# Converting the expert weights piece by piece inside the tile loops, in a transformer layer with 32 routed experts

## The reference

```python
logits = x @ wg.T
scores = softmax(logits)                      # 4096 x 32
weights, idx = top_k(scores, 8)
weights = weights / sum(weights)
# rows sorted by expert, then for each expert e and its rows xs:
g = xs @ w1[e]            # 512 x 192
u = xs @ v1[e]            # 512 x 192
h = silu(g) * u
ys = h @ w2[e]            # 192 x 512
out = zeros().at[token].add(ys * weight)
x = x + layernorm(out)
```

## Time and profile before

| | us |
|---|---|
| median of 3 runs | 2524.11 |
| lowest and highest | 2519.49, 2526.7 |
| the profiled execution, its own time | 2532.36 |
| its span in the trace | 2530.7 |

### The profile page before, as it was taken

The page is one execution under the profiler, slowest core; times in us unless marked ns, Lnnn a source line. Parts: engine busy times, 40 slices in busy tenths (PEclk is TensorE's granted clock), DMA queues, the critical chain, the costliest instruction groups (busy, mean ns, idle before and its releaser), DMA issues.

```text
span 2530.7 us, 62483 instructions
## 1 busy us (share of the span) xinstructions
PE 2255.0 (89%) x11804; PEld 1911.8 (76%) x11805; DVE 1491.3 (59%) x4814; ACT 1228.2 (49%) x2635; POOL 947.9 (37%) x1126
## 2 busy tenths in 40 slices
PE   7999899999989999991798999988999898988990
PEld 5887588888868888880687878867889787977880
DVE  4455567777767777773545555555554555455546
ACT  3343456666556666651334444444444444444443
POOL 1112025555535555556133333323333232323342
PEclk9999999999999999995899999999999999999995
DMA  3234113333333323326798777777787777776778
GB/s 117 91 112 121 59 34 119 105 122 118 122 137 114 127 103 118 116 106 218 209 239 186 149 157 148 158 182 153 150 150 137 166 149 165 138 167 134 137 129 290
DMA packets 164700, 357.53 MB, mean 141 GB/s; under 512 B 21152, under 2 KB 21152, under 8 KB 164512
## 3 DMA queue, kind: packets, MB, share of 16 engines
q0 software_dynamic: 60224, 144.21, 28.9%
q1 hardware_dynamic: 90976, 173.32, 23.1%
q10 hardware_dynamic: 13440, 39.33, 4.8%
HBM read 177.65 MB, written 179.14 MB: 141 GB/s over the span
## 4 chain that ended last, share of the span: by engine, by line
PE 29%; DMA 8%; issue 7%; ACTq 4%; ACT 2%; DVE 2%; DVEq 2%; POOL 1%; SPq 1%; POOLq 0%
DMA moe_sum<-X,aidx 6%; PE bank L443 5%; PE bank L444 5%; PE bank L445 5%; PE bank L434 4%; PE bank L460 2%; PE bank L453 2%; PE bank L464 2%; PE bank L461 2%; PE bank L462 2%; PE bank L463 2%; ACTq L322 1%; ACT WB L500 1%; DMA LATE<-w_in 1%; ACTq L297 1%
## 5 line engine op out<-in xcount | busy, mean ns | idle before, releaser
L1442 POOL DMA_INDIRECT moe_sum<-X,aidx x274 | 425.0, 1551 | 855.9 <-issue 522.5
L922 PE MATMUL bank<-WB,XH 128*128 128x512 f32 x1536 | 478.0, 392 | 0.0
L443 PE MATMUL bank<-WB,XL 128*128 x1096 | 397.7, 363 | 5.0 <-DVE XL L695 4.9
L444 PE MATMUL bank<-WB,XH 128*128 x1096 | 371.6, 339 | 0.0
L445 PE MATMUL bank<-WB,XH 128*128 x1096 | 370.7, 338 | 0.0
L922 PEld LDWEIGHTS bank<-WB,XH 128*128 128x128 f32 x1536 | 290.5, 189 | 60.3 <-issue 0.5
L922 PE MATMUL bank<-WB,XL 128*128 128x512 f32 x768 | 316.5, 412 | 10.4 <-DVE XL L1229 10.4
L922 PE MATMUL bank<-WB,SH 128*128 128x512 f32 x1024 | 318.9, 393 | 0.0
L703 DVE SCALAR_TENSOR_TENSOR BIG<-BIG,bank x274 | 95.2, 347 | 353.8 <-issue 206.5
L1508 POOL DMA_INDIRECT sorted_rows<-srow,pos x256 | 265.4, 1037 | 95.4 <-issue 95.4
L521 ACT ACTIVATE X<-bank (+1 forms) x276 | 165.1, 598 | 224.7 <-PE bank L464 110.4
(11 more groups left out here) (205 smaller groups left out, 4259.4 us busy)
## 6 DMA issues: line engine op xcount, KB each, us to landing
BIG<-sorted_rows SPq DMA_DIRECT2D x276, 274.0 KB
X<-x_in SPq DMA_DIRECT2D x64, 256.0 KB, 2.8
RAW<-w_in ACTq DMA_DIRECT2D x15, 768.0 KB
LATE<-w_in ACTq DMA_DIRECT2D x15, 768.0 KB
sorted_rows<-BIG SPq DMA_DIRECT2D x33, 274.0 KB, 12.7
moe_sum<-LATE SPq DMA_DIRECT2D x34, 256.0 KB, 3.0
LATE<-x_in SPq DMA_DIRECT2D x32, 256.0 KB
RAW<-wo_in SPq DMA_DIRECT2D x16, 512.0 KB, 3.5
```

What stands on the lines that cost most here:

```text
L443: nc.tensor.matmul(eu[s][:, 0:UP], XL[:, s, k, :], wh, start=k == 0, stop=False)
L444: nc.tensor.matmul(eu[s][:, 0:UP], XH[:, s, k, :], wh, start=False, stop=False)
L922: last = nc.tensor.matmul(ps, w, m, start=start and i == 0, stop=stop and i == len(terms) - 1)
L1442: nc.gpsimd.indirect_dma_start(acc_dram[:, :], bass.IndirectOffsetOnAxis(aidx[:, s:s + 1], 0), rows, None, compute_op=ALU.add).then_inc(s_ ...
```

## The change

Each tile of expert e now also converts one piece of 512 columns of expert e+2's weights. The high parts become five pieces of 512 columns (w13 is 1536 columns wide and w2 gives two more pieces), and the layout of a set is such that the low part stands at a fixed distance from the high part. In ACT's tile loop, tile number k within the expert converts piece k & 3, every tile, also when all four have been converted. Behind the loop, ACT runs a second loop over the pieces from m to 4, where m is the smaller of the expert's tile number and 4, then a one-column activation that carries the semaphore `s_ehx`. DVE's tile loop subtracts one piece per tile, and behind its loop it waits for `s_ehx` and for its own pieces (`s_el`), runs a loop over the pieces from m to 3, with m at most 3, and the half piece that carries `s_elo`. Ahead of the tiles stands now `ready`: ACT waits for `s_elo`, issues the load of expert e+3 (three DMAs, since the half piece is loaded once), and waits until the weights of expert e+2 have landed.

The three table entries per expert become one packed word, from which first tile, number and m are taken by shifts. PE reads one word per tile in place of two, and waits before `up` until the low parts of its expert are done.

```diff
@@ each_expert @@
-                n = eng.value_load(table[0:1, 0, bass.ds(e, 1)], min_val=1, max_val=TOKENS // P + 1)
-                first = eng.value_load(table[0:1, 1, bass.ds(e, 1)], min_val=0, max_val=MAX_TILES)
-                convert(e, q)
-                body(e, q, first, n)
+                word = eng.value_load(table[0:1, row, bass.ds(e, 1)], min_val=512 + 32768, max_val=8 * 32768 - 1)
+                first, n, m = word & 511, (word >> 9) & 63, word >> 15
+                ready(e, q)
+                body(e, q, first, n, m)
@@ moe_pe @@
-            def up(g, s, off):
+            def up(g, s, e, off):
+                pe.wait_ge(s_elo, e + 1)
+                stand(pe)
                 pe.wait_ge(s_exl, g + 2)
                 pe.wait_ge(s_h, g + 1)
...
-                    before, now = slot_at(g), slot_at(g + 2)
+                    e, now, before = experts_at(g)
@@ moe_act @@
-            def convert(e, q):
-                if isinstance(e, int) and e + 2 >= EXPERTS:
-                    return
-                load = not (isinstance(e, int) and e + 3 >= EXPERTS)
-                before = act.value_load(table[0:1, 3, bass.ds(e, 1)], min_val=1, max_val=MAX_TILES + 3)
-                act.wait_ge(s_D, before)
-                stand(act)
-                if load:
+            def ready(e, q):
+                if not isinstance(e, int) or e + 3 < EXPERTS:
                     act.wait_ge(s_elo, e + 2)
                     stand(act)
-                for piece in range(len(PIECES)):
-                    weights_high(e + 2, (q + 2) % WSETS, q % 2, piece)
-                    if load and piece < 4:
-                        load_weights(act, e + 3, (q + 1) % 2, piece)
+                    load_weights(act, e + 3, (q + 1) % 2)
+                if converts(e):
+                    act.wait_ge(s_ewr[q % 2], (e - q % 2) * 24 + 96)
+                    stand(act)
...
                     rows_high(g + 2, same)
+                    if converts(e):
+                        weights_high(to, i, (k & (LOW_PIECES - 1)) * PIECE).then_inc(s_eh, 1)
+                with act.Fori(0, n) as k:
+                    tile(first + k, k)
+                if converts(e):
+                    with act.Fori(m, HIGH_PIECES) as k:
+                        weights_high(to, i, k * PIECE)
+                    all_high(e + 2)
@@ moe_dve @@
+                    if converts(e):
+                        dve.wait_ge(s_eh, g + (2 * HIGH_PIECES + 1))
+                        weights_low(to, i, (k & (LOW_PIECES - 1)) * PIECE).then_inc(s_el, 1)
...
+                if converts(e):
+                    dve.wait_ge(s_ehx, e + 3)
+                    stand(dve)
+                    dve.wait_ge(s_el, first + n)
+                    stand(dve)
+                    with dve.Fori(m, LOW_PIECES) as k:
+                        weights_low(to, i, k * PIECE)
+                    last_low(to, i)
@@ tables (DVE) @@
-            nc.vector.tensor_copy(table[:, 0:2, :], tn[0:1, 2:4, :])
-            nc.vector.memset(table[:, 3, 0:1], 1)
-            nc.vector.tensor_scalar(table[:, 3, 1:EXPERTS], tn[0:1, 3, 0:EXPERTS - 1], 3.0, None, ALU.add)
+            done(nc.vector.scalar_tensor_tensor(tn[0:1, 0, :], tn[0:1, 2, :], 512.0, tn[0:1, 3, :], ALU.mult, ALU.add))
+            for i in range(2):
+                done(nc.vector.tensor_scalar(words[:, i, :], tn[0:1, 2, :], float(HIGH_PIECES - 1 - i), 32768.0, ALU.min, ALU.mult))
+            settled()
+            for i in range(2):
+                nc.vector.tensor_tensor(table[:, i, :], words[:, i, :], tn[0:1, 0, :], ALU.add)
...
+            done(nc.vector.tensor_copy(iota_g[0:1, :], bank[6][0:1, 0:MAX_TILES]))
+            settled()
+            nc.vector.scalar_tensor_tensor(at_tile[:, 0, 2:MAX_TILES], iota_g[0:1, 0:MAX_TILES - 2], 64.0, iota_g[0:1, 2:MAX_TILES], ALU.mult, ALU.add)
```

More of the change, by code:

```diff
@@ L487, in moe_pe, with weights_high, all_high @@
             act_t(total - 1, 1)
-            down(total - 2, 0, slot_at(total))
-            down(total - 1, 1, slot_at(total + 1))
+            down(total - 2, 0, experts_at(total)[2])
+            down(total - 1, 1, experts_at(total + 1)[2])
         def moe_act(act):
             act.sem_inc(s_y, 2)
[L495 to L500, removed]
+            def weights_high(q, i, at_piece):
+                return nc.scalar.activation(WB[:, bass.ds(at_piece + q * WSET, PIECE)], raws[i][:, bass.ds(at_piece, PIECE)], ACT.Copy)
+            def all_high(e):
+                nc.scalar.activation(marks[:, bass.ds(e, 1)], mhalf[:, :], ACT.Copy).then_inc(s_ehx, 1)
             def rows_high(g, parity):
@@ L526, in moe_act @@
             act.wait_ge(s_q, 4 * TILES)
-            for piece in range(len(PIECES)):
[L528 to L532, removed]
+            for e in range(2):
+                act.wait_ge(s_ewr[e], 48)
+                for piece in range(HIGH_PIECES):
+                    weights_high(e, e, piece * PIECE).then_inc(s_eh, 1)
+                all_high(e)
+                if e == 0:
+                    act.wait_ge(s_elo, 1)
+                    load_weights(act, 2, 0)
             act.wait_ge(s_T, 3)
@@ L560, in tile @@
                     rows_high(g + 2, same)
-                with act.Fori(0, n) as i:
-                    tile(first + i)
-            total = each_expert(act, convert, body)
+                    if converts(e):
[6 more added lines that the diff above has]
+                    all_high(e + 2)
+            total = each_expert(act, 0, ready, body)
             act_high(total - 1, 1)
@@ L718, in add_index @@
                 nc.vector.tensor_copy(aidx[:, at(0, parity, 1, 1)], BIG[:, bass.ds(tail_at(g) + (WR + ID_COL - W_COL), 1)]).then_inc(s_aid, 1)
-            for piece in range(len(PIECES)):
-                weights_low(1, 1, 1, piece)
+            first_low(1)
             for i in range(2):
@@ L728, in moe_dve, with ready, body, tile @@
                                         ALU.subtract).then_inc(s_exl, 1)
-            def convert(e, q):
-                if isinstance(e, int) and e + 2 >= EXPERTS:
-                    return
-                for piece in range(len(PIECES)):
-                    weights_low(e + 2, (q + 2) % WSETS, q % 2, piece)
-            def body(e, q, first, n):
-                def tile(g):
+            def ready(e, q):
+                pass
+            def body(e, q, first, n, m):
+                to, i = (q + 2) % WSETS, q % 2
+                def tile(g, k):
                     same = g & 1
@@ L743, in tile @@
                     rows_low(g + 2, same)
[L745 to L748 removed]
+                    if converts(e):
+                        dve.wait_ge(s_eh, g + (2 * HIGH_PIECES + 1))
+                        weights_low(to, i, (k & (LOW_PIECES - 1)) * PIECE).then_inc(s_el, 1)
+                with dve.Fori(0, n) as k:
+                    tile(first + k, k)
+                if converts(e):
[6 more added lines that the diff above has]
+                    last_low(to, i)
+            total = each_expert(dve, 1, ready, body)
             act_low(total - 1, 1)
```

92 lines of the change are left out of this document (47 added, 45 removed).

## The result

The changed kernel takes 2560.03 us (median of 4 runs, 2557.08 to 2564.29) beside 2525.4 us for the kernel before in the same session: ratio 1.0135, 95% interval 1.0117 to 1.0152. It is slower, and outside my range.

The account below looks back on a forecast made before the run. PE was taken to bound the expert stage, losing 164 us, partly in gate waits (74.1 us) and half clock (34). Terms +5 +6 +8 -7 -5 -2 = +5, plus 1 for catching up, gave 2530 us; range 2500 to 2556.

Parts of the forecast that it names:

- 18 boundaries behind three tiles or more: Between experts, after one with at least three tiles: gate 0.3 us later at each boundary, +5 us in all.
- 5 behind two tiles: After two-tile experts: one piece more left on each engine and DVE's later start, 1.2 us each, +6 us.
- 6 behind one tile: After one-tile experts: two more DVE pieces, 1.7 us, less a partly vanishing raw-weight wait, 1.4 us each, +8 us.
- rest of the stage: Undisturbed tiles gain 5 us from PE's single word read; 1 us added for tiles being caught up.
- ahead of the first gate: Before the first tile: 3.4 us less ahead of silu, 1.4 us more for DVE's tables, net -2 us.
- The mechanism at the boundary: Between experts: serial chain of DVE's leftover pieces, three ACT issues, silu, gate; 0.3 us later, bounds -0.5 and +1.1.
- The in-loop pieces: In the tile loop: ACT's 0.62 us and DVE's 0.69 us fit into idle time, undisturbed tile stays 3.9 us, cost 0.
- 18 x 0.3: At boundaries after experts with three tiles or more: gate 0.3 us later each, +5 us.
- PE's table word, net -7: Behind stalls on PE: one read less removes 13 us of issue waits, two register steps add 6; bounds -20 and +6.
- short experts and clock cost more: Rival at boundaries: gate 0.8 us later each, nine more half-clock stretches, up to 2555 us; chance 0.16.
- The signs of being wrong: In the profile after: PE's gate waits below 50 us, or the stage's clock off 0.97 by more than 0.01.
- The port: Rival in the tile loop: DVE subtractions and POOL's DMA lock each other out, up to 1.5 us per tile; too-full-loop case 0.05.

Follow-up runs that it names:

- noloop: The changed kernel with no conversion piece inside the tile loop, all pieces behind an expert's last tile: 2617.7 us, ratio 1.0344 to the kernel before.
- before_word: The kernel before with one part of the change alone, PE reading one packed table word per tile in place of two: 2525.23 us, ratio 0.9982.
- four_free: four_ctl with the loads issued ahead of the table read, not behind the wait for the low parts: 2502.06 us, ratio 0.9893 to the kernel before.
- four_copy: four_free with true weights throughout, half the experts' weights copied into internal DRAM during attention and loaded from there: 2503.28 us, ratio 0.989 to the kernel before.
- three_loads: The kernel before with one part of the change alone, three weight loads per expert in place of four: 2516.89 us, ratio 0.9948.
- word_two: before_word with PE reading the packed word twice per tile: 2557.06 us, ratio 1.011 to the kernel before.
- word_wait: before_word with the changed kernel's wait of PE for the low parts added: 2526.32 us, ratio 0.9988 to the kernel before.
- four_rot: four_free with silu one tile ahead on ACT, as in rot: 2535.15 us, ratio 1.003 to the kernel before.
- twowords: The changed kernel with PE reading its packed table word twice per tile: 2630.8 us, ratio 1.0394 to the kernel before.
- four_ctl: The changed kernel with four raw weight buffers, loads still behind the low-parts wait, half the experts loading other bytes: 2561.55 us, ratio 1.0123 to the kernel before.
- rot: The changed kernel with silu moved to the end of ACT's tile steps, one tile ahead: 2580.1 us, ratio 1.0201 to the kernel before.
- split: The changed kernel with four DMA issues per expert in place of three, same bytes: 2577.3 us, ratio 1.0181 to the kernel before.

## Why the prediction was wrong

From the gates of the two profiled executions, in blocks: from an expert's last gate to the sixth gate behind it (or to the last of the next expert, if that is shorter).

| part | predicted | measured |
|---|---|---|
| 18 boundaries behind three tiles or more | +5, less 7 by the word | +15.0 |
| 5 behind two tiles | +6 | +5.9 |
| 6 behind one tile | +8 | +9.4 |
| rest of the stage | -5, +1 | -1.6 |
| ahead of the first gate | -2 | -2.3 |
| behind the last | 0 | +0.4 |
| sum | +6 | +26.8 |

The blocks hold the clock's loss as well, so that +5.9 and +9.4 come so close to their terms is in part luck.

- **The mechanism at the boundary was right.** The chain stands in the trace as written down, with nothing beside it: three issues in a row behind the half subtraction, silu behind them. The in-loop pieces cost an undisturbed tile nothing (3.904 us, noloop), and the stall did not go away.
- **Failed, and the largest part: the sum holds the clock as it was.** I had counted 34 us of loss at the lower level (31.6 by the matmul distances) and then let it stand although the boundaries got longer. It became 16 us more. PE's two columns show this: my terms 5 + 6 + 8 - 7 are 12 us more of idle time, and 12.6 were measured; the busy time I had at -5, and it rose by 16.1. The 12 is a sum of misses in both directions: the wait for the gate rose by 13.9 us, the new wait for the low parts, put at 0 to 6, took 9.4, and waits of kind "issue" fell by 8.6.
- **Failed: "18 x 0.3".** The gate came 0.6 us later than before in the median. At the boundary that I had worked out three joints were too short: into DVE's second loop 0.54 us (I took 0.45), from the half subtraction to the first issue 0.25 (I took none), from the issues to silu 0.74 (I took 0.5, and had 0.8 as a bound). They add 0.6; roundings and steps that I took too long give back 0.3, so the gate stands at XL+7.0 and not 6.7. At 18 boundaries that is +5 us.
- **Failed: "PE's table word, net -7".** Alone it gave 3.3 us. By the same blocks before_word gained the 5 us in undisturbed tiles, and at the boundaries 0.4 in place of 7: I took idle time labelled "issue" for time on the path.
- **The upper end of the range rests on a wrong sum.** The rival "short experts and clock cost more" adds 15 us and 9 x 1.7 us to 2530. That is 2560, not 2555, and 2560 was measured. It is the nearest to what happened, but not by its trigger: three issues took 1.5 us in the median, not over 2. A hit at 2560 would have been luck in part.
- **The signs of being wrong were too coarse.** The gate's wait stayed above 50 us, and the clock's row went from 0.97 to 0.96. A hundredth of the clock over this stage is 12.6 us of time (an estimate, 0.01 x 1261), twice the change that I forecast.
- **Not seen at all:** one issue less than before is worth 13.1 us where issues lie between the pieces. In my sum three issues appear only as a cost. And that the issues come only behind the low parts I took as given; it follows from the two buffers and the place of the loads, and that was the 59.5 us.
- **Two rows misread, without effect on the sum.** The table reads did not fill 2.87 us: 0.59 of that is the high part of the rows, and ACT's idle time is 2.28. And the 30 waits are not one for each of 30 conversions; the stage has 29 boundaries.
- **The port.** By the Trainium skill (SBUF — State Buffer, "SBUF: two separate sides") each in-loop subtraction could have waited for POOL. The trace doesn't show it: 216 of the subtractions of L601 began while POOL's indirect DMA ran; they took 0.68 us in the median and 0.71 at most, like the others, and POOL's instruction kept its 1.55 us.

How stalls and the lower clock go together, for the expert stage of all kernels, in us from the traces. The last column is the sum over matmul distances as above:

| kernel | PE idle over 1.5 us at once | at the lower level | lost by it |
|---|---|---|---|
| four_free | 28.5 | 37.5 | 16.1 |
| four_copy | 29.1 | 41.0 | 16.1 |
| three_loads | 56.4 | 58.0 | 24.3 |
| word_two | 57.9 | 58.0 | 21.4 |
| word_wait | 62.3 | 102.4 | 45.8 |
| four_rot | 71.1 | 99.0 | 40.8 |
| before | 72.5 | 81.9 | 31.6 |
| twowords | 72.7 | 85.3 | 30.3 |
| before_word | 81.2 | 99.0 | 44.0 |
| four_ctl | 88.8 | 109.2 | 47.0 |
| after | 89.1 | 112.6 | 47.9 |
| rot | 105.7 | 157.0 | 58.0 |
| split | 106.3 | 133.1 | 57.0 |
| noloop | 148.6 | 177.5 | 64.1 |

The lower level takes about 1.2 us more for each us of stalls, and about 0.5 us of time are lost with it. But the order is not kept: before_word and word_wait, which change nothing at the boundary but PE's word, lose 12 to 14 us more than before (in the traced executions; over all executions the granted clock differs less, 0.953 and 0.954 against 0.956). So part of the changed kernel's loss may come with the packed word and not with longer stalls. No experiment changed the clock alone; this is a relation and not a proof. four_free's 17 us less of PE busy time against its control (1128.4, 1145.2) come without any change to a matmul.

## What to carry to other kernels

Work that is spread into idle slots doesn't shorten a stall if what releases a buffer, and what is issued then, still sits in a row at its end. Follow the chain across the engines to its last link before you price the pieces, and ask for each link whether another buffer or another order cuts it; when one link is moved, look at what is queued behind it. A stall can cost its length and again the lower clock behind it, here about 0.5 us for each us of stall over all kernels, with much scatter; price both, and check the clock's part against the distances of the matmuls. A removed wait is a gain only if the engine isn't led to the next late one.

## What the runs showed of the hardware

- A second register read on TensorE's queue cost 0.02 us per tile in one loop (before, 3.92 us, against before_word, 3.90) and 0.19 us per tile in another (word_two against before_word), with a few more register steps beside it. In twowords the time shows as longer distances between matmuls (PE's busy time 62 us more), hardly as waits.
- Matmuls of 384 columns began 0.174 us apart at the full clock and 0.320 us apart at the lower level (medians), so the lower level cost a little less than half of PE's speed.
- Three DMA issues in a row took 1.53 us of ScalarE's queue and four took 1.89 us (medians), 0.36 us for one more.
- VectorE's subtractions with two SBUF inputs and GpSimd's indirect DMA ran at once without either taking longer (0.68 and 1.55 us).
- 18.9 MB copied from DRAM to DRAM during attention (DMA share up to the first gate 0.38 with it, 0.33 without) cost nothing that the runs show: first gate at 1220.1 us with it, 1219.9 us without.
